# A transformer layer with product-key experts: layer input added by TensorE, first norm read from a PSUM bank, some work of VectorE, ScalarE and GpSimd in another order

## The reference

```python
x = L0_attn_x                                             # (16, 512, 128)
# attention: rms norm and rope on q and k, causal softmax
out = (softmax(mask(rope(rms(q)) @ rope(rms(k)).T * scale)) @ v).reshape(B, T, C)
x = layernorm(x + out @ w_proj.T)
# experts: 8 heads, 32 x 32 keys, 8 of 1024 experts for each head
xn = rmsnorm(x) * norm_w
s1, i1 = top_k(sim1, 8); s2, i2 = top_k(sim2, 8)          # sim = (xn @ w_q.T) @ keys
fs, pk = top_k(s1[:, None] + s2[None, :], 8); fi = (i1 * 32 + i2)[pk]
hidden = gelu(xn . expert_down[fi]) * relu(fs)
x = layernorm(x + sum(hidden * expert_up[fi]))
```

## Time and profile before

| | us |
|---|---|
| three runs | 1553.46, 1555.92, 1563.68 (median 1555.92) |
| the profiled execution | 1560.93 |
| its span, first to last instruction | 1558.8 |
| busy: TensorE | 1320.8 |
| busy: VectorE | 1373.3 |
| busy: ScalarE | 913.3 |
| busy: GpSimd | 570.6 |

### The profile page before, as it was taken

One profiled execution on the slowest core, in us unless ns is written; L12 is line 12 of the kernel. 1 busy time (PEld: TensorE's weight loads), 2 busy tenths in 40 slices (PEclk: granted clock), 3 DMA queues, 4 the chain that ended last, 5 costly groups with the idle time before them and its releaser, 6 DMA issues.

```text
span 1558.8 us, 55026 instructions
## 1 busy us (share of the span) xinstructions
PE 1320.8 (85%) x20786; PEld 973.5 (62%) x21008; DVE 1373.3 (88%) x6630; ACT 913.3 (59%) x1486; POOL 570.6 (37%) x992
## 2 busy tenths in 40 slices
PE   5675788989898989989898998989888898878677
PEld 4342456666676757666675766667675766556567
DVE  5328799999999999999999999999999999799995
ACT  3565766666666766666666666676766766542110
POOL 4215162351715253361724344261614345040400
PEclk9888999999999999999999999999999999999686
DMA  3000000000000000000000000000000000000000
GB/s 88 8 8 8 8 9 3 15 10 9 16 9 16 10 16 3 9 16 9 16 9 16 9 16 3 9 17 9 16 9 16 3 16 3 2 16 1 9 2 17
DMA packets 30004, 18.80 MB, mean 12 GB/s; under 512 B 1840, under 2 KB 29232, under 8 KB 29744
## 3 DMA queue, kind: packets, MB, share of 16 engines
q1 hardware_dynamic: 29744, 15.23, 3.4%
HBM read 11.04 MB, written 4.19 MB: 10 GB/s over the span
## 4 chain that ended last, share of the span: by engine, by line
PE 58%; ACT 16%; DVE 16%; issue 8%; POOL 2%; ACTq 0%; DVEq 0%; POOLq 0%
PE OV L825 10%; PE G L926 10%; PE G L937 7%; PE F L881 6%; ACT prob L646 6%; PE S L811 5%; PE F L892 4%; PE S L813 4%; PE S L761 3%; DVE onehot L1288 3%; DVE topi L1227 2%; PE F L861 2%; PE S L750 2%; ACT kT_odd L630 2%; ACT stack L608 1%
## 5 line engine op out<-in xcount | busy, mean ns | idle before, releaser
L646 ACT ACTIVATE prob<-S 128x512 f32<-128x512 f32 x640 | 372.1, 596 | 147.9 <-PE S L813 138.1
L926 PEld LDWEIGHTS G<-whot,onehot 128*128 128x128 bf16 x12288 | 364.0, 97 | 82.7 <-issue 41.8
L926 PE MATMUL G<-whot,onehot 128*128 128x16 bf16 x12288 | 382.2, 170 | 22.8 <-DVE whot L1313 17.7
L1288 DVE TENSOR_TENSOR onehot<-lo_no,elo 128x1024 bf16<-128x1024 uint16 x512 | 333.1, 705 | 0.5
L456 POOL TENSOR_TENSOR gat<-qk_r,cosw 128x256 f32<-128x256 f32 x64 | 46.9, 733 | 625.6 <-DVE whot L1313 404.4
L813 PE MATMUL S<-causal,ident_b 128*128 128x128 bf16 x1024 | 198.5, 227 | 50.5 <-ACT prob L646 16.1
L825 PE MATMUL OV<-prob,vp 128*9 128x512 f32 (+3 forms) x2048 | 182.9, 506 | 27.7 <-ACT prob L646 24.2
L575 ACT ACTIVATE hid<-F 128x512 f32<-128x512 f32 x128 | 76.5, 598 | 177.2 <-PE F L881 177.2
L1227 DVE FIND_INDEX8 topi<-topv,sims 128x8 uint16<-128x32 f32 x1024 | 166.2, 186 | 0.0
L825 PEld LDWEIGHTS OV<-prob,vp 128*9 128x9 f32 x2048 | 54.1, 99 | 147.0 <-issue 103.2
L811 PE MATMUL S<-qT,kT_even 128*128 128x384 bf16 (+3 forms) x392 | 96.4, 282 | 53.5 <-ACT prob L646 36.5
(11 more groups left out here) (145 smaller groups left out, 2502.1 us busy)
## 6 DMA issues: line engine op xcount, KB each, us to landing
xa<-in_L_attn_x SPq DMA_DIRECT2D x16, 256.0 KB, 2.8
xr<-in_L_attn_x SPq DMA_DIRECT2D x16, 256.0 KB, 2.8
out<-r SPq DMA_DIRECT2D x15, 256.0 KB, 2.3
onehot<-in_L_ffn_expert_down SPq DMA_DIRECT2D x1, 512.0 KB, 5.2
up<-in_L_ffn_expert_up SPq DMA_DIRECT2D x1, 512.0 KB, 7.5
onehot<-in_L_ffn_keys SPq DMA_DIRECT2D x1, 256.0 KB, 4.5
out<-r SPq DMA_DIRECT2D x2, 128.0 KB, 1.8
onehot<-in_L_attn_w_qkv SPq DMA_DIRECT2D x1, 192.0 KB, 3.0
```

Of the source, the lines that this page charges most:

```text
L646: act.activation(dst, src, ACT.Exp, scale=SCALE).then_inc(exp_done.sem, 1)
L926: last = nc.tensor.matmul(bank[:, 16 * i:16 * i + 16], onehot[:, row, :], whot[:, t, w_part, :], start=(w_part == 0), stop=(w_part == 2))
L1288: return dve.tensor_tensor(onehot[:, row:row + 8, :].rearrange("p t (c i) -> p t c i", i=2), lo, e, ALU.is_equal)
```

## The change

The projection is no longer written to an empty bank. After the turned outputs, step 3 has a new product of TensorE: the unit matrix times the layer input, 128x512 in fp32, into bank A; the projection is then added to it in the bank (`start=False`). VectorE's addition is gone, `r1` is the bank itself, and the statistics, the normalising rows of VectorE and the rows of ScalarE read it there. The turned outputs move from bank A to bank OV, with a signal of their own. Bank A is free again only when ScalarE has read it (`ln1` at 5), and the rows of ScalarE move from step 12 to step 9.

Besides: on VectorE one more one-hot is made ahead of `normalise_o(late, 3)`, and the high rows of quarter 2 are made before `apply_weights(older, 0)` instead of in front of their products. On GpSimd `rests(nxt, 1)` moves behind `gather(late, 0)`. On TensorE the number product of tile 2 moves from step 34 to step 32.

```diff
-        r1 = xr
+        r1 = A
...
-        a_ready = signal("a_ready", 6)
+        a_ready = signal("a_ready", 5)
+        o_turned = signal("o_turned", 1)
...
-        A_USES += [("oTn", [(oTn_done, 1)]), ("proj", [(ln1, 1)])]
+        A_USES += [("proj", [(ln1, 5)])]
...
-        NUMBER_STEPS = [22, 28, 34, 35]
+        NUMBER_STEPS = [22, 28, 32, 35]
...
                 if nxt is not None:
                     rests(nxt, 0)
-                    rests(nxt, 1)
                 if late is not None:
                     gather(late, 0)
                 if nxt is not None:
+                    rests(nxt, 1)
                     third_parts(nxt, 0)
...
             def taken_outputs(b):
-                act.wait_ge(a_ready.sem, a_filled(b, "oTn"))
-                act.activation(oTn[:, :], A[:, :], ACT.Copy).then_inc(oTn_done.sem, 1)
+                act.wait_ge(o_turned.sem, o_turned.value(b, 1))
+                act.activation(oTn[:, :], OV[:, :], ACT.Copy).then_inc(oTn_done.sem, 1)
...
-                    last = act.activation(y_new[:, t, :], r1[:, t, :], ACT.Identity, scale=rs[:, 0, t:t + 1],
+                    last = act.activation(y_new[:, t, :], r1[:, t * P:(t + 1) * P], ACT.Identity, scale=rs[:, 0, t:t + 1],
...
-                    if n == 12 and late is not None:
+                    if n == 9 and late is not None:
                         norm1_rows(late)
...
                 if g == 0:
                     pe.wait_ge(v_done.sem, v_done.value(b, 1))
+                    if not (isinstance(b, int) and b == 0):
+
+                        pe.wait_ge(oTn_done.sem, oTn_done.value(b - 1, 1))
...
+            def input_first(b):
+                pe.wait_ge(xr_loaded.sem, xr_loaded.value(b, 16))
+                wait_a_empty(pe, b, "proj")
+                nc.tensor.matmul(A[:, :], ident[:, :], xr[:, :, :].rearrange("p t d -> p (t d)"), start=True, stop=False,
+                                 skip_group_check=True)
+
             def turn_outputs(b):
                 pe.wait_ge(o_done.sem, o_done.value(b, NG))
-                wait_a_empty(pe, b, "oTn")
+                pe.wait_ge(oT_done.sem, oT_done.value(b, NG))
                 for t in range(NT):
-                    last = nc.tensor.transpose(A[:, t * P:(t + 1) * P],
+                    last = nc.tensor.transpose(OV[:, t * P:(t + 1) * P],
                                                o[:, t].rearrange("p h d -> p (h d)"), ident[:, :])
-                last.then_inc(a_ready.sem, 1)
+                last.then_inc(o_turned.sem, 1)
...
             def project_out(b):
                 pe.wait_ge(oTn_done.sem, oTn_done.value(b, 1))
-                wait_a_empty(pe, b, "proj")
                 for t in range(NT):
                     last = nc.tensor.matmul(A[:, t * P:(t + 1) * P], oTn[:, t * P:(t + 1) * P], wprojT[:, :],
-                                            start=True, stop=True)
+                                            start=False, stop=True, skip_group_check=True)
...
                             turn_outputs(late)
+                            input_first(late)
...
             def norm1_moments(b):
 
                 dve.wait_ge(a_ready.sem, a_filled(b, "proj"))
-                dve.wait_ge(xr_loaded.sem, xr_loaded.value(b, 16))
-                dve.tensor_tensor(r1[:, :, :].rearrange("p t d -> p (t d)"), A[:, :],
-                                  xr[:, :, :].rearrange("p t d -> p (t d)"), ALU.add).then_inc(ln1.sem, 1)
-                moments(r1, 0, ln1, b)
+                dve.sem_inc(ln1.sem, 1)
+                moments(r1[:, :].rearrange("p (t d) -> p t d", t=NT), 0, ln1, b)
...
-                one_hots(hot(8, 10))
+                one_hots(hot(8, 11))
                 if late is not None:
                     normalise_o(late, NG - 1)
-                one_hots(hot(10, 16))
+                one_hots(hot(11, 16))
...
                 if older is not None:
+                    high_rows(older, 2)
                     apply_weights(older, 0)
...
                 if older is not None:
-                    weighted_one_hots(older, 2)
+                    weighted_one_hots(older, 2, high=False)
```

More of the change, by code:

```diff
@@ L1174, in norm1 @@
                 for t in range(NT):
-                    last = dve.tensor_scalar(yi[:, t, :], r1[:, t, :], mv[0][:, t, 0:1], rs[:, 1, t:t + 1],
+                    last = dve.tensor_scalar(yi[:, t, :], r1[:, t * P:(t + 1) * P], mv[0][:, t, 0:1], rs[:, 1, t:t + 1],
                                              ALU.subtract, ALU.mult)
@@ L1293, in one_hots, with high_rows @@
                     one_hot(n)
-            def weighted_one_hots(b, quarter):
+            def high_rows(b, quarter):
                 pair, t0 = quarter // 2, quarter % 2 * 64
@@ L1307, in weighted_one_hots @@
                                   ALU.is_equal).then_inc(hi_done.sem, 1)
+            def weighted_one_hots(b, quarter, high=True):
+                pair, t0 = quarter // 2, quarter % 2 * 64
+                if high:
+                    high_rows(b, quarter)
+                dims = [P, 64, NHI, 2]
+                hot = hot_hi[:, :, :].rearrange("p t (c i) -> p t c i", i=2)
                 dve.wait_ge(hi_done.sem, hi_done.value(b, quarter + 1))
```

## The result

| | before | after |
|---|---|---|
| median of four runs, us | 1555.97 | 1581.53 |
| lowest and highest of after | | 1577.99 and 1584.37 |
| the profiled execution of after | | 1577.99 (span 1576.2) |
| mean granted clock of TensorE | 0.921 | 0.906 |

The change makes the kernel slower: the ratio is 1.0141, with a 95% interval of 1.0114 to 1.0167. Forecast were 1541 us and a range of 1524 to 1559. The time lies 22.5 us above the range.

What follows compares the result with a forecast made beforehand. TensorE was taken to bound the usual turn, VectorE 0.45 us behind. There +0.92 - 1.5 - 0.56 = -1.14; with turns taken as 87.25 against 88.35, twelve save 13 us, others 2: 1555.9 - 15 = 1541 us, range 1524 to 1559.

Steps and rivals of the forecast that it cites:

- The product, +0.92 in full: TensorE's added unit matrix by layer input, ahead of the projection: all counts, +0.92 us a turn (bounds 0.90 and 1.1).
- VectorE's savings in X worth nothing: Step 31 to next turn's first chunk: VectorE's dropped addition and moved work gain 0, since TensorE sets the pace.
- The reserve at the first chunk: VectorE ready at about 741.5 for the first expert weights chunk, due from TensorE at 742.4: near 0.9 us spare.
- The new pause of VectorE at chunk 3: Sign: VectorE, now earlier, starts to wait some tenths of a us for TensorE's chunk 3 of expert weights.
- ScalarE's relief, -1.5: Norm rows moved to step 9 shrink TensorE's pauses of 1.07 and 1.33: -1.5 us a turn (bounds 0.5 and 1.6).
- The comparison of line 1249, -0.7: VectorE's first comparison, 1.79 us beside GpSimd's subtractions, loses most of the overlap: -0.7 us (bounds 0 and -0.96).
- The number product, -0.56: Third tile's product, moved from step 34 to 32, fills TensorE's pause for ScalarE's copy of keys: -0.56 us.
- Slower by the delayed copy at step 9, 1569: Rival: ScalarE's rows at step 9 delay its copy of the attention sums, relief lost: +13 us, 1569; chance 0.08.
- Half clock on other work, 1552: Rival: TensorE's half rate falls on other work, seven us more each turn, undoing most gain: 1552; chance 0.22.
- Y: Stretch from first expert weights chunk to step 31, where both engines race: TensorE 42.1 to 40.6, VectorE 41.6 to 40.2.
- Full clock, 1537: Rival: smaller TensorE pauses make its half-rate stretches vanish, turns 87.1 or 86.9, 16 to 20 us saved: 1537; chance 0.20.
- VectorE in charge with all of its savings arriving, 1518: Rival: VectorE bounds the kernel and all it saves arrives, 2.8 us a turn, 38 us: 1518; chance 0.10.

Runs made afterwards that it cites:

- the kernel after moved by 240: The changed kernel with 240 never executed instructions ahead of TensorE's loop, its closing branch at instruction 7362: 1540.99 us, ratio 0.9884 to the kernel before.
- the kernel with the rows alone: The kernel before with only ScalarE's four rows of the first norm moved from step 12 to step 9: 1559.29 us, ratio 1.0003.
- 7314: Place of the closing branch in the changed kernel moved by 192 never executed instructions ahead of TensorE's loop: 1538.31 us, ratio 0.9866 to the kernel before.

## Why the prediction was wrong, point by point

**The step that failed.** The prediction defined X as the stretch from step 31 "over the loop's edge to the first chunk of the next turn" and changed in it only the product: "+0.92 in X", what follows "is paced by TensorE as before". The edge itself has no term, no bound and no rival. It was taken as unchanged, and it was the only place that changed much. For each of the eleven taken branches it costs 2.3 us of pause and 0.9 us of half clock behind it, 36 us in all; the loop as a whole is 39 us longer. The trace of before showed the branch at 0.357 us and could not have shown what it costs four instructions further on. But the body of the loop on TensorE did get longer, and that a branch has a price that might depend on its place was a rival to be named: one mechanism, one place, with the sign of slower.

**The sum without the edge.** With the branch at a quick place the changed kernel takes 1540.99 and 1538.31 us; the forecast was 1541. The ratios are 0.9884 and 0.9866 where 1541 stands for 0.9904, so 18 to 21 us are saved and not 15; that the first of the times meets the forecast to the microsecond is luck. Seen from VectorE the turns alternate, as VectorE's timeline of the kernel after moved by 240 shows:

```profile
797.39 0.89 DVE L1163 BATCH_NORM_STATS2 stats<-A 128x6 f32<-128x128 f32 x4 [1.53 <-DVEq L1175]
...
883.98 0.89 DVE L1163 BATCH_NORM_STATS2 stats<-A 128x6 f32<-128x128 f32 x4 [0.50 <-DVEq L1175]
...
971.47 0.89 DVE L1163 BATCH_NORM_STATS2 stats<-A 128x6 f32<-128x128 f32 x4 [1.54 <-DVEq L1175]
```

They last 86.6 and 87.5, the mean of the two is 87.04, and the forecast was 87.25. From branch to branch all eleven take 87.0 to 87.1. In the short one TensorE waits for VectorE; its timeline, the same kernel:

```profile
854.48 0.76 PE L936 MATMUL G<-whot,onehot 128*128 128x16 bf16 x24 [0.91 <-DVE whot L1332]
```

That is the two-runner picture of the prediction. The granted clock is 0.98 in the short turn and 0.94 in the long one; before it was 0.94. In the kernel as changed, the short kind of turn also fits: 88.6 less its pause of 1.40 at the edge is 87.2.

**The terms.**
- The product, +0.92 in full: right, 0.86 in place, and all of it arrives (11.5 and 14.2 us, by the kernel compared with, of 13.8).
- VectorE's savings in X worth nothing: right. The pause at the projection is 1.53 (1.5 to 2 forecast). The reserve at the first chunk was put near 0.9 and is 0.35: VectorE gets there later than I had it, by half a microsecond, of which reading the bank (below) explains up to 0.3. The pause at the turned sums was to fall below 0.3 and is 0.65 here; it is TensorE's own pause of 1.41 at the edge, a few products earlier, that comes through. In the kernel after moved by 240, where the edge costs nothing, VectorE has no pause in front of these sums, as forecast. The new pause of VectorE at chunk 3, the last of the signs, doesn't appear in either kernel.
- ScalarE's relief, -1.5: the pauses fell from 2.40 to 1.04, which is -1.36, and the rows fit. What it brings by itself is 0, because VectorE takes over and the half rate moves to X; together with VectorE's part it is 24 us, 1.4 a turn from branch to branch. The prediction counted on both and said that VectorE stood 0.45 behind. By its own row, 781.20 and 2.01, the weighted rows end at 783.21 and not at 783.10, so it is 0.34; the order of the two holds.
- The comparison of line 1249, -0.7: right, from 1.79 to at most 0.98.
- The number product, -0.56: about right, 0.7 a turn from branch to branch.

**The rivals.** Slower by the delayed copy at step 9, 1569: the sign came out, the mechanism didn't; ScalarE has 0.90 to spare there. Half clock on other work, 1552: seen behind the pause at the edge, and in the kernel with the rows alone, where it moves from Y to X. Full clock, 1537: seen in part, in every other turn of the kernel at 7362 (0.98). VectorE in charge with all of its savings arriving, 1518: not seen.

**The rule on operands in PSUM.** By the row of the tile yi in the kernel after, VectorE's normalising instruction takes 0.402 us from the bank:

```profile
L1184 DVE TENSOR_SCALAR yi<-A,mv,qk_rs x64: 397/402/412, 123.6 to 1461.4; 128x128 f32<-128x128 f32 x64
```

In the kernel before, the same tile from SBUF:

```profile
L1175 DVE TENSOR_SCALAR yi<-xr,mv,qk_rs x64: 339/342/348, 124.0 to 1442.0; 128x128 f32<-128x128 f32 x64
```

The price is 0.06 us each, 0.24 a turn, and four statistics rows take 0.89 in place of 0.87. The Trainium skill ("VectorE: DVE Perf Modes", section "Why PSUM operands drop a tier") had led to an estimate of 0.8 us a turn for both; by the rows it is 0.26, and the measurement decides. It changed neither the sum nor the result.

## What to carry to other kernels

When a change adds or removes instructions on an engine that runs a loop on the chip, read the row of the loop's closing branch before and after, ahead of any other reading; if it has grown, put never executed instructions ahead of the loop until it is quick again and the loop's first products run without a second pause, and judge the change only then. Count the records, too, before comparing busy times: 222 missing products made 25 us here. Compare two versions at equally quick places: here four instructions of place weigh 2.4%, more than every other edit of this study. Where two engines race through a stretch, relieve both at once, and don't move work from the one that waits to the one that is waited for: the version that left the addition on VectorE and took all the rest is the fastest, at 0.978.

## What the runs showed of the hardware

The closing branch of TensorE's loop costs 3.71, 3.28 or 2.96, 1.09, 0.44 and 0.357 us (medians) at 4, 16, 80, 144 and 208 or more instructions behind the edge that lies between instructions 7106 and 7110. Where the taken branches are quick (7106 and 7362), there is a pause of 3.02 and 3.36 us behind the one that isn't taken, at the loop's exit; at 7314 it is 0.47, 49 instructions later. A loop that starts 16 to 20 instructions ahead of such an edge pauses once more in each turn, for 1.05 to 2.24 us, just where the edge lies. A pause of TensorE of 3.31 us was followed by a granted clock of 0.50; over the eleven edges the products behind the pauses took 10 us more, two fifths of the 26 us of pause. ScalarE reads the bank faster than SBUF here: its four rows take 1.50 us from bank A and took 1.64. What stays open is what part the prefetch hint has in it, and why the pause at the edge is 1.4 us in some turns and 3.3 in others while the branch stands in one place; no run was made for either.
